# Two graph attention layers on one core: in layer 1, the probabilities times V of tiles 0 to 2 as one part of 384 columns instead of two of 192, and all four output projections in the second chunk

## The reference

```python
# layer 0: bias and mask from adj, softmax over keys, residual
h = relu(layernorm(x)); q, k, v = heads(h @ Wq + bq), heads(h @ Wk + bk), heads(h @ Wv + bv)
scores = where(adj > 0, q @ k.T / sqrt(32) + beta * adj, -9e15)
x = x + softmax(scores) @ v
# layer 1: the same with other weights, bias = 2 * adj, and an output projection
h = relu(layernorm(x)); q, k, v = heads(h @ Wq.T), heads(h @ Wk.T), heads(h @ Wv.T + bv)
p = softmax(q @ k.T * 384 ** -0.5 + (adj + adj))        # rows of zeros give zeros
x = x + (p @ v) @ Wo.T + bo
```

## Time and profile before

| | before |
|---|---|
| median of 3 runs | 2079.84 us (2074.91 to 2080.26) |
| the profiled execution | 2086.44 us, its span 2084.7 us |
| PE busy | 1945.9 us, 93% |
| DVE busy | 1863.5 us, 89% |
| ACT busy | 1641.0 us, 79% |
| DMA packets | 419.04 MB, mean 201 GB/s |

### The profile page before, as it was taken

One profiled execution on the slowest core, in us unless ns is written; L12 is line 12 of the kernel. 1 busy time (PEld: TensorE's weight loads), 2 busy tenths in 40 slices (PEclk: granted clock), 3 DMA queues, 4 the chain that ended last, 5 costly groups with the idle time before them and its releaser, 6 DMA issues.

```text
span 2084.7 us, 49577 instructions
## 1 busy us (share of the span) xinstructions
PE 1945.9 (93%) x18240; PEld 1255.6 (60%) x18240; DVE 1863.5 (89%) x4056; ACT 1641.0 (79%) x4151; POOL 859.6 (41%) x1051
## 2 busy tenths in 40 slices
PE   5999999999999999897999999999999999999995
PEld 3666556656565666564666666666666666666663
DVE  4999999999999999998989888998889988898883
ACT  4998888888888988887878777777778777777771
POOL 6355554444555554432334233433334333443321
PEclk9999999999999999999999999999999999999997
DMA  3878879987788889887878778877878778777775
GB/s 128 199 205 217 221 197 233 235 221 209 201 221 224 215 222 238 218 214 210 207 198 217 181 181 203 207 194 182 198 187 216 185 180 206 192 201 188 169 177 142
DMA packets 105105, 419.04 MB, mean 201 GB/s; under 512 B 27216, under 2 KB 30800, under 8 KB 104864
## 3 DMA queue, kind: packets, MB, share of 16 engines
q1 hardware_dynamic: 77920, 307.60, 58.9%
q0 software_dynamic: 26944, 108.27, 19.2%
HBM read 88.61 MB, written 25.17 MB: 55 GB/s over the span
## 4 chain that ended last, share of the span: by engine, by line
PE 49%; DVE 29%; DMA 8%; ACT 6%; SPq 4%; issue 3%; POOL 0%; DVEq 0%; POOLq 0%
DVE s L340 15%; PE ring L241 13%; PE sc L219 11%; DVE pt L353 10%; PE out L292 9%; DMA pk<-pt 8%; PE ring L266 6%; PE ring L248 5%; SPq L180 4%; ACT s L465 3%; PE ring L230 2%; ACT pl L487 2%; DVE wo L386 1%; DVE hT L364 1%; PE ring L257 1%
## 5 line engine op out<-in xcount | busy, mean ns | idle before, releaser
L465 ACT ACTIVATE s<-s,nmax 128x512 f32<-128x512 f32 x1536 | 1094.2, 727 | 294.5 <-DVE nmax L340 293.8
L340 DVE CUSTOM_DVE_ANT_0 s<-sc,bias 128x512 f32<-128x512 f32 x1536 | 968.4, 686 | 66.9 <-PE sc L219 46.3
L353 DVE STREAM_TRANSPOSE pt<-s 128x2048 f32<-128x2048 f32 x288 | 663.9, 2305 | 3.6 <-issue 3.6
L219 PE MATMUL sc<-k,q 32*128 32x512 f32 x3072 | 443.4, 647 | 69.0 <-DVE nmax L340 61.0
L292 PE MATMUL out<-pk,v 128*32 128x192 f32 x6144 | 298.7, 337 | 35.5 <-DMA pk<-pt 35.5
L465 ACT ACTIVATION_READ_ACCUMULATOR s<-s,nmax 128x1 f32 x1536 | 312.0, 203 | 0.0
L292 PEld LDWEIGHTS out<-pk,v 128*32 128x32 f32 x6144 | 183.5, 112 | 186.0 <-issue 94.4
L248 PE MATMUL ring<-wv,hT 128*128 128x384 f32 x1152 | 236.7, 350 | 0.0
L219 PEld LDWEIGHTS sc<-k,q 32*128 32x128 f32 x3072 | 123.4, 185 | 183.4 <-DVE nmax L340 110.3
L241 PE MATMUL ring<-hT,wq 128*128 128x512 f32 x864 | 229.2, 410 | 1.5 <-DVE hT L364 1.5
L241 PE MATMUL ring<-hT,wk 128*128 128x512 f32 x864 | 229.0, 409 | 1.5 <-ACT q L497 1.5
(11 more groups left out here) (81 smaller groups left out, 1834.1 us busy)
## 6 DMA issues: line engine op xcount, KB each, us to landing
pk<-pt SPq DMA_DIRECT2D x1536, 192.0 KB, 6.0
bias<-in_adj POOLq DMA_DIRECT2D x32, 1024.0 KB, 12.2
res<-in_x POOLq DMA_DIRECT2D x16, 768.0 KB, 15.4
x_between<-res POOLq DMA_DIRECT2D x16, 768.0 KB, 10.5
xin<-x_between POOLq DMA_DIRECT2D x16, 768.0 KB, 10.1
res<-x_between POOLq DMA_DIRECT2D x16, 768.0 KB, 10.9
out_x<-res POOLq DMA_DIRECT2D x16, 768.0 KB, 7.6
xin<-in_x POOLq DMA_DIRECT2D x15, 768.0 KB, 9.3
```

The lines of the kernel that those rows point to most:

```text
L219: mm = nc.tensor.matmul(m.sc[:, j, :], m.q[rows, s % 2, P * t:P * (t + 1)], m.k[rows, s % 2, :], start=True, stop=True)
L340: nc.vector.tensor_tensor_reduce(out=m.s[:, t % 2, j, :], in0=m.sc[:, j, :], in1=m.bias[g % 2][:, t, :], scale=s_scale[layer], scalar=3.0e ...
L353: nc.vector.transpose(out=to, in_=m.s[:, t % 2].rearrange("p j (i a e) -> p (j i) a e", a=QUADS, e=HD)).then_inc(turned, 1)
L465: nc.scalar.activation(tile, tile, ACT.Exp, bias=m.nmax[s % 2][:, t, j:j + 1], scale=-1.0, accum_out=m.sums[s % 2][:, t, j:j + 1]).then_in ...
```

## The change

In layer 1 `pv` of tiles 0 to 2 becomes one part. It waits for both halves of the transfers and has 16 matmuls of 384 columns instead of 32 of 192. It stands at t = 0 of the step after, where the second half stood; at t = 2 there is none any more. The fourth output projection, `("post", g - 1, 3)`, moves from the first place of the third chunk to the third place of the second. `parts_done` turns the counts of parts into those of two a step in layer 1, for all who wait for them. Layer 0 keeps its three parts.

```diff
@@ in_step, the table of layer 1
-            (1, 2): [("post", g - 1, 2)],
+            (1, 2): [("post", g - 1, 2), ("post", g - 1, 3)],
-            (2, 0): [("post", g - 1, 3)],
@@ pv_in_step
     s = DT * g + c - (2 if t == 0 else 1)
-    return (*chunk(s), (2, 0, 1)[t]) if s >= 0 else None
+    part = (2, 0, 1)[t] if s < DT * B else (1, 0, None)[t]
+    return (*chunk(s), part) if s >= 0 and part is not None else None
+
+def parts_done(s, part):
+    first = min(s, DT * B)
+    return PARTS * first + 2 * (s - first) + (part if s < DT * B else min(part, 1)) + 1
@@ move (SP)
-                        sp.wait_ge(pv_ready, PARTS * (s - 1) + half + 2)
+                        sp.wait_ge(pv_ready, parts_done(s - 1, 1 + half))
@@ pv (PE)
-                    pe.wait_ge(moved[layer_of(g)][c][part - 1], MOVES * (g % B + 1))
-                    quads = slice(part - 1, QUADS, HALVES)
+                    halves_of = (part - 1,) if layer_of(g) == 0 else range(HALVES)
+                    for half in halves_of:
+                        pe.wait_ge(moved[layer_of(g)][c][half], MOVES * (g % B + 1))
+                    quads = slice(part - 1, QUADS, HALVES) if layer_of(g) == 0 else slice(0, QUADS)
@@ the last steps (PE)
-            pv(GRAPHS - 1, DT - 2, HALVES)
+            pv(GRAPHS - 1, DT - 2, 1)
             pv(GRAPHS - 1, DT - 1, 0)
             for x in CLOSING:
                 if x[0] == "post" and x[2] == 0:
                     pv(GRAPHS - 1, DT - 1, 1)
-                    pv(GRAPHS - 1, DT - 1, 2)
                 item(*x)
```

More of the change, by code:

```diff
@@ L395, in scale_out @@
                 dve.wait_ge(done["spread"], nth("spread", g, c))
-                dve.wait_ge(pv_ready, PARTS * (DT * g + c + 1))
+                dve.wait_ge(pv_ready, parts_done(DT * g + c, PARTS - 1))
                 nc.vector.tensor_tensor(m.oT[:, c, :], m.out[:], m.rspread[:], ALU.mult).then_inc(pv_done, 1)
@@ L485, in item @@
                     if j == 0 and s:
-                        act.wait_ge(pv_ready, PARTS * (s - 1) + 1)
+                        act.wait_ge(pv_ready, parts_done(s - 1, 0))
                     nc.scalar.activation(m.pl[:, j, :], frm, ACT.Copy).then_inc(done["tp"], 1)
@@ L520, in copy_out @@
             def copy_out(g, c):
-                act.wait_ge(pv_ready, PARTS * (DT * g + c + 1))
+                act.wait_ge(pv_ready, parts_done(DT * g + c, PARTS - 1))
                 nc.scalar.activation(m.oT[:, c, :], m.out[:], ACT.Copy).then_inc(pv_done, 1)
```

## The result

The changed kernel takes 2122.72 us (median of 5 runs, 2114.09 to 2149.5); the kernel before, in runs beside it, 2079.84 us (median of 5). The ratio of the times is 1.018 (95% interval 1.0156 to 1.0203), which leaves out the slowest run, 2149.5 us. That is slower by 37 us by the ratio and by 43 us by the medians, where 20 were forecast.

A forecast was written before the change was run, and what follows sets the result against it. The prediction took PE's own order to set layer 1's pace. 0.51 us a graph plus 0.5 for transfers made 1.0; 15.5 graphs x 1.0 + 4.5 at the end = 20 us on 2079.8, so 2100 us, range 2086 to 2124.

The forecast's parts named there:

- The first place: First place of each step: wide part takes 2.72 us, 1.29 us more, filling the 0.34 us waits of chunks 0 and 1.
- The third place: Third place of chunks 0 and 2: PE loses a 1.44 us part, then waits 0.80 us for ACT's copy of k.
- The sum without transfers: Layer 1, chunks 0, 2 and 1 together: + 0.31, - 1.42 and + 1.62 us, + 0.51 us a graph.
- The transfers' wait: Chunk 0's interval: 20.8 us between wide parts against PE's 20.34, so PE waits about 0.5 us a graph for moved blocks.
- The clock: Within the transfers' upper bound, 3.8 us: as in layer 0, where the clock falls to 0.61 of full after the wait.
- The end: End of the kernel: last 16 transfers begin 2 us later and more PE work follows their landing, + 4.5 us.
- The moved projection costs nothing by itself: Fourth output projection: chunk 1 pays 2.1 us, chunk 2 gets 2.1 us back.
- The saving of the join: Wide part in layer 1: 2.72 us against 1.43 + 1.44 for two, saving 0.15 us a step, 0.45 a graph.
- (a): Rival: the transfers are the bound, 2 to 3 us a graph more, 2131 to 2146 us; chance 0.22.
- (b): Rival: faster, k's copy found ready and transfers landing in time, - 13 us, 2067 us; chance 0.08.
- (c): Rival: no measurable change, parts save 0.9 us and transfers land in time, + 5 us; chance 0.1.
- (d): Rival: the sum without the transfers' wait, 12 us, 2092 us; counted in the likeliest case, chance 0.6.

The follow-up runs named there:

- kcover: Changed kernel with part 0 (tile 3, 128 columns) moved from t = 1 to t = 2 in layer 1, before the scores that need k: 2119.1 us, ratio 1.0148.
- resq: Changed kernel with layer 1's residual load cut to the first of four tiles, so the result lacks a part: 2101.11 us, ratio 1.0062.
- again: The changed kernel run and profiled once more, with no edit: 2132.69 us, ratio 1.0201 to the kernel before.
- halves_t0: Changed kernel's order without the join: two parts of 192 columns at the first place, each waiting for its own half: 2099.05 us, ratio 1.008.
- halves_t0_kcover: As halves_t0, with part 0 (tile 3) moved to t = 2 to cover k: 2084.75 us, ratio 0.9994.
- oldposts: Changed kernel with the fourth output projection back at the first place of chunk 2: 2137.82 us, ratio 1.026.
- kcover_resq: Changed kernel with both edits, part 0 at t = 2 and layer 1's residual load cut to a quarter: 2087.55 us, ratio 1.0018.

## Why the prediction was right or wrong

**The direction and the new waits were right,** and so were most sizes on PE. 2122.72 us lies at the upper edge of the range, and the sum had about half of the loss. By the prediction's own sign (waits for `pk` over 1.5 us a graph) one term was wrong: they were 1.95 and 1.58 us in the two profiles, not 0.5.
- *The first place.* 2.72 us forecast for the wide part, 2.71 measured; the 0.34 us waits went.
- *The third place.* 0.80 us forecast for k, 0.78 measured, 24 times. DVE is through with the scores 0.3 us before k is there (1421.70 against 1421.97), where 0.4 was forecast. Once k is covered DVE is the releaser (kcover, 0.42 us).
- *The sum without transfers.* + 0.51 us a graph forecast, + 0.55 in resq, where PE has no wait for the blocks. The close agreement is in part luck: 20.34, 26.50 and 20.34 us were forecast for chunks 0, 1 and 2, and 20.48, 26.05 and 20.48 are measured in resq (medians of 14 graphs), 0.32 us a graph above before. Most of chunk 1's difference is the projection that comes in: behind another it adds 1.82 us (the two take 3.96, one took 2.14), not 2.1.

**The transfers' wait was mis-sized, by a row read one transfer short.** The step "17.9 us from first issue to last landing, with one load of 768 KB beside it" ends with a transfer issued at 1436.65. That is the fifteenth of the row; the last two lines of the earlier trace rows are not the last two of the step. The row and its last two transfers:

```profile
1426.01 11.87 SPq L180 DMA_DIRECT2D pk<-pt  x16
...
L180 SPq DMA_DIRECT2D pk<-pt x2: 590/590/591, 1436.7 to 1437.3; - x2
...
DMA to landing us min/median/max: 7.2/7.8/8.4
```

The sixteenth is issued at 1437.29 and takes 8.4 us: 1437.29 + 8.4 - 1426.0 = 19.7 us. With it the interval is 2.72 + 0.1 + 19.7 + 0.1 = 22.6 us, PE's wait against 20.34 is 2.3 us, and the sum is 15.5 x 2.8 + 4.5 = 48 us, which is 2128, above the range. The changed kernel's row, issued from 1410.8 behind the wide part, agrees:

```profile
L186 SPq DMA_DIRECT2D pk<-pt x2: 507/550/592, 1410.8 to 1411.4; - x2
...
L186 SPq DMA_DIRECT2D pk<-pt x1: 598/598/598, 1421.6 to 1421.6; - x1
...
DMA to landing us min/median/max: 9.6/9.6/9.6
```

1421.6 + 9.6 - 1410.8 = 20.4 us. Over the graphs of layer 1 such a row with a 768 KB load beside it takes 18.1 to 20.0 us in the kernel before (13 graphs, median 18.9) and 18.3 to 20.5 us in the changed one (14 graphs, median 19.3). In the changed kernel's chunk 2, where the load is through within 1.6 us of the row's start, the row takes 15.3 to 15.9 us. So the kernel before held the right price. PE's waits vary from 0.79 to 2.95 us as the row does; why it varies by 2 us from graph to graph with the same order is open.

**The clock was named as a bound and left out of the sum.** The fall to 1.2 GHz behind some of the waits of 2 to 3 us adds about 0.5 us a graph. Together: "again" is 2.66 us a graph above before, of which 0.55 are the orders of PE and DVE (resq), about 1.6 the wait for the blocks and about 0.5 the clock. 15.7 graphs (47 steps) of 2.66 are 42 us. My + 1.0 would have given 16.

**The end** was forecast at + 4.5 us; the five kernels with the wide part and the new projections show + 5.1 to + 8.6, halves_t0 and halves_t0_kcover, with two parts, - 1.9 and + 1.4. What was missing is a wait for the row before the last one. The last 16 transfers were to begin 2 us later; counted from the last start of `ring<-ksum,q` they begin 23.3 us behind it instead of 16.3, and PE had just waited for the row before them:

```profile
2107.72 4.41 PE L301 MATMUL out<-pk,v 128*32 128x384 f32 x32 [4.20 <-DMA pk<-pt]
```

Single executions of this end differ by some microseconds, and the clock changes several times in it.

**"The moved projection costs nothing by itself"** was too simple. It gains 0.6 us a graph beside the wide part (oldposts). I had read that place on PE alone and had not followed what DVE's `scale_out` waits for. The move by itself, in the kernel before, was not run.

**The saving of the join was credited to the wrong thing.** 0.15 us a step is what two parts at two places cost more than one; halves_t0 shows that two parts back to back save it as well (2.73 against 2.71 us). Fewer and wider matmuls brought 0.02 us of themselves here, and my reading of the rows, 0.15, was wrong. By the 2.5 ns for each matmul beside its columns that the Trainium skill gives for isolated matmuls (TensorE: Matmul & The Clock Gate, Back-to-back issue gap), 16 matmuls fewer on four strips are an estimated 0.01 us; the 0.02 us measured agree with that size.

**The rivals.** (a), the transfers as the bound with 2 to 3 us a graph more, is half true: 1.1 us more in waits than the 0.5 of the sum, and 0.5 us of clock, 25 us in all. (b) is refuted: even without the waits for k and for the blocks (kcover_resq) the kernel is level with before. DVE then releases PE instead, in 60 waits of 0.42 us each. (c), no change, is refuted by the time. (d), the sum without the transfers' wait, is what resq shows: 12 us forecast, 13 by its ratio.

## What to carry to other kernels

Joining two parts joins their waits: the row of transfers behind one buffer then starts later and must be complete sooner, and the time between is what to compare with the row. Count the transfers of a row before taking its length, and read it in every graph: here the sixteenth was missed, and it was 1.8 us of the 2.3 us that decided. Before taking a piece of work out of a place, look at what ran under it on the other engines; a 1.4 us part covered a 0.8 us copy and a DVE 0.4 us behind it. And where an engine's small items wait for the bound engine, put the long work that waits for nothing ahead of them: this alone gave 0.7% here, and with two split parts at one place and k covered, 1%, two figures whose intervals overlap.

## What the runs showed that I had not expected

A wait of 2 to 3 us inside an otherwise full stretch of TensorE can cost more than itself: the 32 rows behind it took 4.48 us at the lower clock instead of 2.79, in "again" behind a wait of 1.97 us already. The length of the wait alone does not decide, since kcover kept the full clock behind one of 2.72 us; what else does is not shown. The mean granted clock goes with the time of the changed kernel's executions: 0.985 at 2114.09 us, 0.984 at 2120.56, 0.982 at 2127.03, 0.976 at 2149.5. The transfers' row with a load beside it varied from graph to graph by over 2 us though each graph issues the same. And 64 matmul rows of 192 columns took 0.02 us more than 32 of 384.
